# Where the spill of a split W2 chunk stands on SyncE's queue, and where its split stands on GpSimd, in a cross-attention and expert kernel

## The reference

```python
x = x + attention(ctx, ctx, layernorm(x), mask)        # q, k, v, o projections with biases
h = layernorm(x)
xn = h * rsqrt(mean(h * h) + 1e-6) * rms_w
expert = argmax(softmax(xn @ gate_w.T))                # one of 8 for each token
out = x + top_score * (silu(xn @ W1[e] + b1[e]) @ W2[e] + b2[e])
```

## Time and profile before

| | us |
|---|---|
| median of 3 runs | 913.38 |
| lowest and highest | 910.83, 922.73 |
| the profiled execution, its own time | 916.12 |
| its span in the profile | 914.4 |
| granted TensorE clock over the span | 0.957 of full speed |

### The profile page before, as it was taken

The page is one execution under the profiler, slowest core; times in us unless marked ns, Lnnn a source line. Parts: engine busy times, 40 slices in busy tenths (PEclk is TensorE's granted clock), DMA queues, the critical chain, the costliest instruction groups (busy, mean ns, idle before and its releaser), DMA issues.

```text
span 914.4 us, 28096 instructions
## 1 busy us (share of the span) xinstructions
PE 786.0 (86%) x8532; PEld 561.5 (61%) x8532; DVE 566.1 (62%) x1870; ACT 436.4 (48%) x1039; POOL 518.0 (57%) x727
## 2 busy tenths in 40 slices
PE   2579999999999999998999888985288998987994
PEld 2346666666666666656666555653177877865773
DVE  4256777777777777667666665764644555542542
ACT  1246666666666666655665655643043232231330
POOL 0476776776677675677656775564235544645311
PEclk9979999999999999999999999997589999998998
DMA  4285786677577577656776567741522222222200
GB/s 111 85 220 151 181 198 182 175 194 198 158 193 207 149 197 200 204 153 178 187 205 195 153 193 182 198 120 37 211 72 78 72 70 67 88 66 75 51 29 7
DMA packets 103383, 130.08 MB, mean 142 GB/s; under 512 B 12989, under 2 KB 89943, under 8 KB 102808
## 3 DMA queue, kind: packets, MB, share of 16 engines
q1 hardware_dynamic: 97176, 116.38, 47.2%
q0 software_dynamic: 5600, 12.87, 4.7%
q10 hardware_dynamic: 544, 0.00, 0.0%
HBM read 94.07 MB, written 36.06 MB: 142 GB/s over the span
## 4 chain that ended last, share of the span: by engine, by line
PE 66%; issue 8%; POOL 7%; SPq 6%; DMA 6%; DVE 4%; ACT 1%; POOLq 0%; DVEq 0%; ACTq 0%
PE ps L1281 12%; PE ps L1301 11%; PE ps L1089 6%; PE ps L1071 6%; PE ps L1105 6%; PE ps L1075 5%; PE ps L1119 5%; DMA w_spill<-arena_b 4%; PE ps L1140 3%; PE ps L1049 3%; POOL arena_w L628 3%; PE ps L1168 2%; POOL arena_b L634 2%; SPq L500 2%; SPq L495 2%
## 5 line engine op out<-in xcount | busy, mean ns | idle before, releaser
L809 ACT ACTIVATE arena_b<-ps 128x448 f32<-128x448 f32 (+1 forms) x384 | 194.2, 540 | 131.8 <-PE ps L1075 131.5
L1443 DVE CUSTOM_DVE_ANT_0 arena_w<-ps,arena_w 112x375 bf16<-112x375 f32 x256 | 140.3, 548 | 92.9 <-PE ps L1049 89.4
L1071 PE MATMUL ps<-arena_b,arena_w 128*128 128x448 bf16 x384 | 137.7, 359 | 11.3 <-DVE arena_b L1452 10.0
L1443 DVE CUSTOM_DVE_ANT_0 arena_b<-ps,arena_w 112x375 bf16<-112x375 f32 x256 | 139.9, 546 | 0.0
L1075 PE MATMUL ps<-arena_b 128*128 128x224 f16 x768 | 137.2, 260 | 0.0
L950 ACT ACTIVATE arena_b<-ps,b_sb 128x256 f32<-128x256 f32 (+1 forms) x176 | 63.4, 430 | 152.1 <-PE ps L1281 118.1
L1281 PE MATMUL ps<-arena_b,w_parts 128*128 128x256 f16 (+1 forms) x1056 | 111.8, 254 | 6.5 <-issue 6.2
L1301 PE MATMUL ps<-arena_w,arena_b 128*128 x840 | 105.8, 281 | 13.4 <-issue 12.7
L1281 PEld LDWEIGHTS ps<-arena_b,w_parts 128*128 x1056 | 90.1, 98 | 24.4 <-issue 11.1
L1301 PEld LDWEIGHTS ps<-arena_w,arena_b 128*128 128x128 f16 x840 | 82.8, 100 | 33.2 <-issue 20.9
L1075 PEld LDWEIGHTS ps<-arena_b 128*128 128x128 f16 x768 | 75.7, 99 | 42.5 <-issue 1.6
(11 more groups left out here) (205 smaller groups left out, 1281.4 us busy)
## 6 DMA issues: line engine op xcount, KB each, us to landing
arena_b<-k_spill SPq DMA_DIRECT2D x128, 192.0 KB, 3.9
arena_b<-in_L_ffn_W SPq DMA_DIRECT2D x64, 256.0 KB, 4.5
arena_b<-q_spill SPq DMA_DIRECT2D x128, 112.0 KB, 4.3
k_spill<-arena_b SPq DMA_DIRECT2D x32, 384.0 KB, 3.4
arena_b<-in_ctx SPq DMA_DIRECT2D x32, 375.0 KB, 4.9
arena_w<-in_x SPq DMA_DIRECT2D x64, 112.0 KB, 4.6
q_spill<-arena_w SPq DMA_DIRECT2D x32, 224.0 KB, 2.1
rows<-arena_w SPq DMA_DIRECT2D x32, 224.0 KB, 2.3
```

The costliest lines, as they stand in the source:

```text
L809: nc.scalar.activation(probsT[u % PROB_BUFFERS][0:n], scoreT_bank[c][0:n, 0:QUAD * T], ACT.Exp, scale=1.0 / SCALE_SCORES).then_inc(probs_r ...
L1071: pe.matmul(bank[:, 0:QUAD * T], mask_keys[:, quad, c, :], max_rows[par].rearrange("p h t -> p (h t)"), start=True, stop=False)
L1443: nc.vector.tensor_tensor_reduce(out=masked_scores[r % 2], in0=shared_bank[r][0:T, 0:S], in1=mask_bias, scale=-1.0, scalar=3.4e38, op0=ALU ...
```

## The change

Two things move. On SP the write of the W2 chunk no longer stands after `x_tail` of the next step; it stands in the step of its own split, between `k_spill` and `q_spill`, and waits there for the split of the same batch. On POOL `split_w2` moves from before `residual` to the end of the step, behind the second `context_low`. SP's loops now turn where the others do (at batch 16 and not 17), and `route_constants` waits for the last split by a semaphore.

```diff
@@ SP, step
                     b = st.batch(1)
                     wait_apart(sp, res_ready, b, sp_passed)
                     sp.dma_start(x_tail, x[bass.ds(b, 1)].rearrange("o t d -> t (o d)")).then_inc(x_tail_loaded, 16)
-
-                    if st.base - 1 >= DIRECT:
-                        wait_apart(sp, w2_split_ready, b + 1, sp_passed)
-                        sp.dma_start(w2_spill[:, bass.ds(b - DIRECT, 1), :, :].rearrange("p o s n -> p s (o n)"),
-                                     w2_split).then_inc(w2_spilled, 16)
...
                     sp.dma_start(k_spill[par].rearrange("s p n -> p s n"),
                                  k_parts[par].rearrange("p s j k -> p s (j k)")).then_inc(k_spilled, 16)
+                if st.exists(0) and st.base >= DIRECT:
+
+                    b = st.batch(0)
+                    wait_apart(sp, w2_split_ready, b + 1, sp_passed)
+                    sp.dma_start(w2_spill[:, bass.ds(b - DIRECT, 1), :, :].rearrange("p o s n -> p s (o n)"),
+                                 w2_split).then_inc(w2_spilled, 16)
+                if st.exists(-1):
+
+                    b, par = st.batch(-1), st.parity(-1)
                     wait_apart(sp, q_stacked[par], Q_MOVED * st.half(-1), sp_passed)
...
-            run_steps(sp, step, PEELED_FIRST + 1, DIRECT + 1)
+            run_steps(sp, step, PEELED_FIRST, DIRECT)
@@ POOL, route_constants
+                pool.wait_ge(w2_split_ready, B)
@@ POOL, step
                     queries_rstd(st.batch(-2), st.parity(-2))
-                if st.exists(0):
-                    split_w2(st)
                 if st.exists(1):
                     residual(st)
...
                     context_low(st.batch(-2), st.parity(-2), 1)
+                if st.exists(0):
+                    split_w2(st)
```

## The result

| | before | changed |
|---|---|---|
| median | 914.93 us (4 runs, 910.83 to 922.73) | 944.58 us (4 runs, 941.24 to 945.83) |
| profiled execution, its own time | 916.12 | 945.83 |
| its span | 914.4 | 944.0 |

The changed kernel takes 1.031 times as long (95% interval 1.026 to 1.036). The forecast was 944.

The account below looks back on a forecast made before the run. It took the second half to be bound by a loop through POOL and SP, 18.98 us a step, growing to 21.1. Loops +27 and end +3 gave +30 us: 946 profiled, 943.4 from the median, stated as 944; range 928 to 957.

Parts of the forecast that it names:

- The mechanism: Late steps: SP's write waits for the split, x_tail stands behind it, residual waits for x_tail; first half unchanged.
- The loop: Late steps: split's end to write, q_spill, x_tail, residual and the next split's end; 21.1 us a step against 18.98.
- The sum up to step 28: Late steps: +3.6 us at step 17 and +23.5 over eleven loops, together +27.
- the start: First half, 16 steps: the change adds nothing, taken as 0; TensorE keeps 17.5 us a step.
- Steps 29 and 30: Ctx and x no longer loaded, context_low ends; loop under 18 us, TensorE sets the pace, the 27 us kept.
- The end: Last batches: route_constants behind the last split delays routed_factor and the last add_residual, to 661 us; +3 us.
- x_tail's landing: Late steps: issue of x_tail to residual 4.48 us, plus 0.3 for the write's 256 KB ahead of it.
- lower bound of the loop: Late steps: loop 20.5 us, no shift by the write and 0.6 instead of 0.95; +20 us, 933 us.
- upper bound: Late steps: loop 22.2 us, the full 0.97 and q_stack 0.4 late; +43 us, 957 us.
- Fast landing: Rival, late steps: x_tail lands after its minimum of 2.1 us, loop 18.7 us, 911 us in all; chance 0.08.
- The clock: Rival, late steps: idle TensorE loses granted clock; two falls make 21.6 us a step, about 950 us; chance 0.10.
- rival B of e1: Late steps: TensorE's clock makes them long; with TensorE not idle the clock stays up, 897 us; no chance given.
- The collision of the write: Rival, late steps: the write's 256 KB delay the loads behind it, the upper bound, 957 us; chance 0.07.

Follow-up runs that it names:

- e3: Against the changed kernel, on SP: x_tail of batch s loaded in step s, right ahead of the chunk's write; 873.15 us, ratio 0.984 to the kernel before.
- e9: Against the changed kernel, on SP: q_spill moved ahead of the waiting chunk write, x_tail still behind it; 905.84 us against 887.62, ratio 1.020 to the kernel before.
- e1: Against the changed kernel, on POOL: split_w2 back ahead of residual, the write's new place kept; 872.01 us against 886.33, ratio 0.983 to the kernel before.
- e2: Against the kernel before, on POOL: split_w2 last in the step, the chunk's write left behind x_tail of the next step; 873.08 us, ratio 0.984.
- e4: Against the changed kernel, on SP: x_tail issued later, behind the two W loads of its step; 931.85 us against 886.33, ratio 1.051 to the kernel before.
- e8: Against the changed kernel, on SP: x_tail issued sooner, ahead of ctx and x; 918.27 us against 911.5, ratio 1.006 to the kernel before.
- e6: The changed kernel run again without any edit, beside the kernel before; 937.80 us, ratio 1.029 to the kernel before.
- e7: The kernel before, unchanged, profiled in one run on this chip; late step 18.90 us, residual of step 16 at 331.50 us.
- e5: Against the changed kernel, on POOL: the routing's constants made one step earlier, in step 31 behind split_w1; 938.02 us, ratio 1.030 to the kernel before.

## Why the prediction was right, and where its terms were off

**The mechanism.** Each step of it stands: the wait for the landed write went; SP waited 10.8 us a step for the split ("10 us or more"); residual waited 90.2 us in twelve steps ("some 90 us"); the residuals of steps 17 and 28 stand 226.7 us apart (232 said, 208.8 before); the first half kept its step (17.43 us from residual to residual in steps 5 to 15, 17.40 before). TensorE waits for mask_queries (L632) in each of these eleven steps, but for context_low (L638) in seven only. e3 and e9 show that x_tail is the link, e1 and e2 that both moves are needed, e4 and e8 that the loop follows x_tail's issue.

**The loop, 21.1 predicted, 20.61 measured.** The turn shown takes 20.92 us, the mean of the eleven 20.61. In that mean: from the split's end to the write 0.24 (0.3 predicted), to q_spill 0.57 (0.65), to x_tail 6.75 (6.95; it is 6.90 in the turn shown, and some 6.63 in every other, as from 345.75 to 352.38), to residual 4.80 (4.48 + 0.3), residual to the split's end 8.25 (8.45). Every term is within 0.2 us, and all but the landing were a little high. Eleven turns of 0.5 us make 5.5 us too much.

**The sum up to step 28, +27 predicted, +23.2 measured** (583.74 against 560.56). 1.7 of the 23.2 are the start, which the prediction had at 0 and which e6 and e7 show to be chance. So the loop gave 21.5, of it 3.5 at step 17 (3.6 predicted).

**Steps 29 and 30: the step of the prediction that failed.** It said that ctx and x are no longer loaded from step 29 on, that context_low ends, that the loop falls under 18 us and TensorE keeps the pace. Residual took 19.92 and 19.52 us, against 17.03 and 17.99 before, which adds 4.4 us. Ctx and x are gone, as it said. But context_low is of batch s + 2 and still runs in step 29, in both its parts. SP's queue, then POOL, in step 29:

```profile
592.64 0.36 SPq L540 DMA_DIRECT2D q_spill<-arena_w  x1
...
597.84 1.34 SPq L512 DMA_DIRECT2D arena_w<-in_x  x1
```

```profile
603.66 0.64 POOL L645 TENSOR_TENSOR arena_w<-arena_w 112x256 f32<-112x256 f32 x1 [7.02 <-DMA arena_w<-in_x]
604.26 1.12 POOL L638 TENSOR_TENSOR arena_b<-arena_b 128x512 f16<-128x512 f32 x1
...
608.14 0.63 POOL L638 TENSOR_TENSOR arena_b<-arena_b 128x238 f16<-128x238 f32 x1
...
610.84 1.09 POOL L623 TENSOR_TENSOR arena_b<-arena_b 128x512 f16<-128x512 f32 x1
```

From residual to the split's end POOL takes 8.27 us in step 29, as in the loop; only in step 30 is it 6.60, and residual of step 31 follows that of step 30 after 16.8 us. The prediction's own 21.1 less the two issues of ctx and x (1.2) is 19.9, close to both measured steps: what brought it under 18 was POOL's work taken off one step too soon (it had the splits of steps 28 and 29 end 18.1 us apart; they end at 591.99 and 611.93, 19.9 apart). The second term that was off is x_tail's landing. With ctx and x gone, x_tail is issued 5.2 us behind q_spill in step 29 and 5.0 in step 30, but residual starts 5.8 and 5.65 us after it and not 4.8: from q_spill to residual 11.0 and 10.6 us, against 11.55 in the loop's mean. In e8, where ctx and x stand behind x_tail, it was 9.7 us in the turn shown; why the two differ was not tried. The issue of x_tail also took 1.34 us in step 29 instead of 0.33.

**The end, +3 predicted.** The last add started 27.6 us later than before (658.75 against 631.11). TensorE's product was ready at 656.58, against 631.06 before: 25.5 us later, so of the 4.4 us that residual lost in steps 29 and 30 only 2.3 reach it, 0.65 of them in the product itself (2.10 us instead of 1.45). The rest, 2.2 us, is the hold by the constants. VectorE waited 4.96 us for routed_factor:

```profile
658.42 0.41 DVE L1465 TENSOR_SCALAR arena_w<-arena_w,arena_b 112x256 f32<-112x256 f32 x1 [4.96 <-POOL arena_b L654]
```

That they hold this add is shown; that 2.2 us would be won without them is not (e5). Another 2.0 us come from the expert phase (285.3 us behind that add against 283.3), which the change doesn't touch; on the chip of e6 and e7 the same stretch took 277.4 us in the changed kernel and 278.8 in the kernel before, so the change does not lengthen it.

**The total.** Measured are 21.5 (step 17 and the loop) + 1.7 (start) + 2.3 (steps 29 to the last product) + 2.2 (constants) + 2.0 (expert phase) = 29.7 us; predicted were 27 + 0 + 0 + 3 + 0 = 30. That 944 met 944.6 to the microsecond is luck: the loop was sized 5.5 us too high, and what was put at nothing came to 6.0. The forecast also started from a median of 913.4, which is 914.9 with the fourth run. And its lower bound of the loop leaves out the +3 of the end that its upper bound has: 3 + 16.5 + 3 is +22, 936 and not 933; the range stated is wider than either.

**The rivals.** Fast landing: x_tail's landing did not fall to 2.1 us. The prediction's estimate of 2.3 us (the Trainium skill, DMA: Bandwidth & Descriptors, "Anatomy of one DMA") comes from a fit made on DMAs that GpSimd issues. X_tail is issued by SP, and the measurement decides: in steps 18 to 28 of the changed kernel's first trace, e4 and e8 residual starts 4.2 to 5.2 us after its issue. The clock: more falls came, as that rival expected (nine of the eleven late steps have a granted clock of 0.92 or 0.83, where before one in eleven is under 1.00). They did not lengthen the steps, because the loop is longer than TensorE's step with the loss in it (0.92 over 20.5 us is 1.6 us lost), and this answers rival B of e1 too. Residual to residual took 20.65, 20.75 and 20.31 us in the steps that begin at 419.19, 439.84 and 460.59, and their granted clock was 0.83, 1.00 and 0.83 (columns of the earlier trace rows):

```profile
419.20:439.80 20.60, 18.17 (x182) 11.38 (x175) 11.35 (x40) 9.95 (x24) 12.34 (x18) 0.83 0.64 171
439.80:460.60 20.80, 19.10 (x239) 12.76 (x237) 14.64 (x55) 13.14 (x32) 12.41 (x19) 1.00 0.63 166
460.60:480.90 20.30, 17.39 (x169) 11.03 (x169) 11.27 (x40) 9.39 (x21) 12.35 (x18) 0.83 0.64 170
```

The collision of the write: the landing is 4.80 us in the mean, 0.3 above the 4.48 of the first half; no run tells whether the write's bytes are the cause.

## What to carry to other kernels

A wait on SP's in-order queue costs by what stands behind it (8 us of waiting a step cost nothing in e3, 10.8 cost 3.1 us a step in the changed kernel): list the loads behind it, and look for one that the awaited engine itself needs, since then the two close a loop whose length is the step. Two moves that each take an operation off such a loop can together make a longer one, so try them one by one: here the write in the step of its split, with the split left early, takes 872 us where the kernel before takes 886 (ratio 0.983, against 1.03 for both moves). Where a load is waited for in every step, its place in the order of issues is the cheap thing to change.

## What was not expected

The kernel before takes some 25 us less in two of the four comparisons, and in the traces of those it is the expert phase that is shorter: from the last residual add to the end it is 283 and 285 us in the first two traces, 277 to 279 in e5 to e8, and 253 to 255 in e1 to e4 and e9. A window of that phase (columns as above), first the changed kernel in its first comparison, then e1 on another chip:

```profile
760.00:780.00 20.00, 17.59 (x156) 14.95 (x154) 11.05 (x22) 6.28 (x16) 8.75 (x9) 1.00 0.18 52
```

```profile
760.00:780.00 20.00, 20.00 (x185) 17.83 (x184) 13.06 (x24) 7.25 (x18) 12.34 (x11) 1.00 0.27 79
```

TensorE gets through 185 matmuls instead of 156 at the same clock, with no idle time. In the slower traces the groups of instructions put that idle time down to "issue", where no engine or DMA is waited for (18.9 us before the matmuls of L1307 alone in the changed kernel's, against 0.1 in e1). The first half of the step phase is equally long in both (17.43 and 17.41 us a step, steps 5 to 15). What differs between the chips was not tested.
